# Weight sums of batch 0 on GpSimd, x turned in another order, gate inverses in step 0

## What is computed

```
xn = layernorm(x)
q, k, v = xn @ Wq.T, xn @ Wk.T, xn @ Wv.T      # 32 query heads, 8 key/value heads, 128 wide
q, k = rmsnorm(q) * q_norm_w, rmsnorm(k) * k_norm_w
attn = softmax(q k^T / sqrt(128) + alibi bias, causal)      # 4 query heads share a key head
s = (attn v) @ Wo.T
g = silu(xn @ W.T + bias + lora part)
out = x + s * g
```

## Time and profile before

| | |
|---|---|
| median of 3 runs | 2909.21 us (2906.86 to 2913.39) |
| the profiled execution | 2908.81 us, span 2906.9 us |
| TensorE busy, weight loads | 2658.3 us (91%), 2341.4 us (81%) |
| VectorE, ScalarE, GpSimd busy | 1741.1 (60%), 1771.0 (61%), 1684.1 us (58%) |
| HBM traffic | 151 GB/s over the span |
| granted TensorE clock, mean | 0.963 of full speed |

### The profile page before, as it was taken

How to read it: one execution, slowest core, us unless ns; L and a number is a source line. 1 busy time by engine, 2 the same in 40 slices (tenths; PEclk the granted TensorE clock), 3 DMA queues, 4 the chain that set the end, 5 groups by cost and what they waited for, 6 DMA issues and landing times.

```text
span 2906.9 us, 39948 instructions
## 1 busy us (share of the span) xinstructions
PE 2658.3 (91%) x13840; PEld 2341.4 (81%) x13840; DVE 1741.1 (60%) x3544; ACT 1771.0 (61%) x4627; POOL 1684.1 (58%) x821
## 2 busy tenths in 40 slices
PE   3668888888989999999989999999999999999997
PEld 2557777777878888888878888888877888888886
DVE  4445665556555666556656675655566575555566
ACT  2255555545666666666666666667666666766663
POOL 3366556656655576665555666566555665655643
PEclk8879999999999999999999999999999999999999
DMA  7767556665634433333423443333422543333323
GB/s 246 248 213 236 209 185 228 230 210 177 237 110 137 143 124 109 118 115 114 144 86 114 144 129 110 120 114 105 144 89 86 179 131 115 106 112 115 110 83 120
DMA packets 184119, 424.48 MB, mean 146 GB/s; under 512 B 34544, under 2 KB 75632, under 8 KB 183024
## 3 DMA queue, kind: packets, MB, share of 16 engines
q1 hardware_dynamic: 183920, 421.93, 44.4%
HBM read 349.51 MB, written 89.13 MB: 151 GB/s over the span
## 4 chain that ended last, share of the span: by engine, by line
PE 74%; DVE 8%; DMA 5%; ACT 5%; POOL 4%; SPq 3%; issue 3%; POOLq 0%; DVEq 0%; ACTq 0%
PE proj L477 18%; PE proj L479 17%; PE proj L478 17%; PE tr L570 4%; PE sc L477 3%; DMA wu<-xtok 3%; PE sc L478 2%; PE sc L479 2%; PE ot L478 2%; PE ot L479 2%; PE tr L550 2%; PE ot L477 2%; POOL wl L913 2%; SPq L295 1%; DVE pT_lo L1093 1%
## 5 line engine op out<-in xcount | busy, mean ns | idle before, releaser
L913 POOL TENSOR_TENSOR wl<-wl,wh 128x896 fp32r<-128x896 f32 x448 | 986.9, 2232 | 720.6 <-ACT wh L696 720.4
L477 PE MATMUL proj<-wh,xh 128*128 128x448 f32 x1792 | 679.9, 379 | 84.3 <-POOL wl L913 59.7
L478 PE MATMUL proj<-wl,xh 128*128 128x448 f32 x1792 | 665.6, 371 | 0.0
L479 PE MATMUL proj<-wh,xl 128*128 128x448 f32 x1792 | 665.2, 371 | 0.0
L924 POOL TENSOR_TENSOR wb_lo<-wb_lo,wb_hi 128x1024 fp32r<-128x1024 f32 x128 | 307.8, 2404 | 414.2 <-ACT wb_hi L706 414.2
L763 ACT ACTIVATE prob<-prob,negmax 128x128 f32<-128x128 f32 (+3 forms) x512 | 286.6, 564 | 339.9 <-DVE negmax L1128 339.9
L1150 DVE TENSOR_TENSOR acc<-acc,proj 128x512 f32<-128x512 f32 x480 | 327.5, 683 | 216.1 <-PE proj L479 214.4
L696 ACT ACTIVATE wh<-wl 128x896 fp32r<-128x896 f32 x448 | 406.8, 964 | 79.3 <-DMA wl<-wu 79.1
L477 PEld LDWEIGHTS proj<-wh,xh 128*128 128x128 f32 x1792 | 342.6, 191 | 123.6 <-issue 67.7
L477 PE MATMUL proj<-o_hi,wb_hi 128*128 128x512 f32 x1024 | 428.4, 418 | 12.3 <-issue 6.1
L479 PE MATMUL proj<-o_hi,wb_lo 128*128 128x512 f32 x1024 | 407.2, 398 | 0.0
(11 more groups left out here) (121 smaller groups left out, 4498.0 us busy)
## 6 DMA issues: line engine op xcount, KB each, us to landing
wl<-wu SPq DMA_DIRECT2D x448, 448.0 KB, 3.9
wb_lo<-wo_in SPq DMA_DIRECT2D x128, 512.0 KB, 3.3
wu<-xtok SPq DMA_DIRECT2D x98, 448.0 KB, 4.4
wo_in<-wo SPq DMA_DIRECT2D x32, 512.0 KB, 5.5
xtok<-wa SPq DMA_DIRECT2D x56, 256.0 KB, 4.1
gate_dram<-z_buf SPq DMA_DIRECT2D x32, 256.0 KB, 5.1
xtok<-wa SPq DMA_DIRECT2D x56, 128.0 KB, 4.1
xtok<-xT SPq DMA_DIRECT2D x28, 256.0 KB, 5.2
```

Of the source, the lines that this page charges most:

```text
L477: pe.matmul(out, hi_l, hi_r, start=first, stop=False, skip_group_check=onto)
L478: pe.matmul(out, hi_l, lo_r, start=False, stop=False, skip_group_check=onto)
L479: return pe.matmul(out, lo_l, hi_r, start=False, stop=last, skip_group_check=onto)
L913: pool.tensor_tensor(w_slot(wl, w), w_slot(wl, w, True), w_slot(wh, w), ALU.subtract).then_inc(w_ready, 1)
```

## The change

Four edits, all of them of order and place; the amount of TensorE's work stays.

1. The weight sums of half 0 in the steps pass from VectorE to GpSimd, into step j=1 ahead of the low parts of P4 and P5. On SP, `store_sums`, the landing wait and the twelve loads now stand ahead of `load_product` in j=0 and j=2, `store_halves` ahead of it in j=1.
2. x: another order of the fills and other sums (P6's goes to r21 rather than r22, and P5, P3 read it there), fills 0 to 3 in (6,3), 4 to 9 in (7,0), 10 to 13 in (7,1), some of them behind quarters of the output product; `x_sum` stands around `low_b` in (7,0) and (7,1). VectorE takes each fill's low part a piece later.
3. Layer norm: for batches 2 and 3 statistics and factors a group earlier, all four scalings in (6,1); x is loaded in g=3. For batch 1 two scalings move behind P3's pieces in (6,3).
4. Gate: the four inverses in j=0 (in j=1 for g=7 with a batch to come), the product always in j=1. `store_result(·, 0)` goes from j=2 to j=1, `finish` ahead of the low parts.

```
-FILLS = [P4, P1, P2, P6, P7, P5, P3]
-FILL_AT = {P1: (0, 0), P2: (0, 512), P4: (2, 512), P7: (2, 0), P6: (2, 512), P5: (0, 0), P3: (0, 512)}
+FILLS = [P1, P2, P7, P4, P6, P5, P3]
+FILL_AT = {P1: (0, 0), P2: (0, 512), P7: (2, 0), P4: (2, 512), P6: (2, 0), P5: (0, 0), P3: (0, 512)}
...
-    at = {(6, 3): range(0, 4), (7, 0): range(4, 8), (7, 1): range(8, 12), (7, 2): range(12, 14)}
+    at = {(6, 3): range(0, 4), (7, 0): range(4, 10), (7, 1): range(10, 14)}
...
+def ln_group(b):
+    return 6 if b == 1 else 5
```

On SP, in `step` at j = 0:

```
-                    load_product(n + 1, P6)
-                    load_product(n + 1, P7)
                     if new is not None:
                         sp.wait_ge(prep_tst[1], 64 * new)
                         load_weights(new, 0)
                         load_gate_weights(new, 0)
+                    load_product(n + 1, P6)
+                    load_product(n + 1, P7)
```

At j = 1:

```
-                    load_product(n + 1, P4)
                     if new is not None:
                         store_halves(new, 0)
+                    load_product(n + 1, P4)
+                    if g == 0 and ending is not None:
+                        store_result(ending, 0)
                     load_product(n + 1, P5)
```

At j = 2:

```
-                    if g == 0 and ending is not None:
-                        store_result(ending, 0)
-                    load_product(n + 1, P3)
...
                     if new is not None:
                         store_sums(new, 0)
                         sp.wait_ge(prep_tst[0], 64 * (new + 1))
                         load_weights(new, 1)
                         load_gate_weights(new, 1)
+                    load_product(n + 1, P3)
```

At j = 3:

```
-                    if g == 5 and 0 < b < BATCH - 1:
+                    if g == 3 and 0 < b < BATCH - 1:
                         load_x(b + 1)
```

On TensorE, in `turn_x` and `step`:

```
-                    pe.wait_ge(ln_ready, 4 * b + (2 if p == P4 else 4))
+                    pe.wait_ge(ln_ready, 4 * b + (4 if p == P4 else 2))
...
                 if v >= 0:
                     out_ready(v)
-                    out_proj(v, 0)
-                    out_proj(v, 1)
+                    for c in range(2):
+                        out_proj(v, c)
+                        if fills:
+                            turn_x(fills.pop(0))
```

On ScalarE, in `step`:

```
-                if (g, j) == (6, 3) and b + 1 < BATCH:
-                    ln_scale(b + 1, 0)
-                    ln_scale(b + 1, 1)
...
+                    if (g, j) == (6, 3) and b == 0 and u[1] == P3:
+                        ln_scale(1, 2 + u[2])
...
+                while fills:
+                    x_hi(fills.pop(0))
+                if (g, j) == (6, 1) and 0 < b < BATCH - 1:
+                    for t in range(NT):
+                        ln_scale(b + 1, t)
                 for k in range(3):
                     probs_hi(m, k)
-                if (g, j) == (6, 1) and b + 1 < BATCH:
+                if (g, j) == (ln_group(b + 1), 1) and b + 1 < BATCH:
                     ln_rsqrt(b + 1)
-                if (g, j) == (6, 2) and b + 1 < BATCH:
-                    ln_scale(b + 1, 2)
-                    ln_scale(b + 1, 3)
+                if (g, j) == (6, 2) and b == 0:
+                    ln_scale(1, 0)
+                    ln_scale(1, 1)
```

On GpSimd, in `step`:

```
                 bias_of(m + 1)
+                if next_x is not None:
+                    if (g, j) == (7, 0):
+                        x_sum(next_x, P7)
+                    if (g, j) == (7, 1):
+                        x_sum(next_x, P5)
                 low_b(v + 1)
+                if next_x is not None:
+                    if (g, j) == (7, 0):
+                        x_sum(next_x, P6)
+                    if (g, j) == (7, 1):
+                        x_sum(next_x, P3)
                 if j == 0:
                     values_lo(n)
-                if (g, j) == (6, 3) and b + 1 < BATCH:
-                    x_sum(b + 1, P7)
-                if j == 3 and n + 2 < HKV:
-                    weight_sums(n + 2)
-                low_product(*[(n + 1, P6), (n + 1, P4), (n + 1, P3), (n + 2, P1)][j])
-                if (g, j) == (6, 3) and b + 1 < BATCH:
-                    x_sum(b + 1, P6)
-                if (g, j) == (7, 0) and b + 1 < BATCH:
-                    x_sum(b + 1, P5)
-                if (g, j) == (7, 1) and b + 1 < BATCH:
-                    x_sum(b + 1, P3)
+                if j in (1, 3) and n + 2 < HKV:
+                    weight_sums(n + 2, j // 2)
                 if g == 0 and b > 0 and j in (1, 3):
                     finish(b - 1, j // 2)
+                low_product(*[(n + 1, P6), (n + 1, P4), (n + 1, P3), (n + 2, P1)][j])
```

On VectorE, in `step` (with `late_gate = g == 7 and next_x`):

```
                 for i, u in enumerate(pieces):
                     p, t = u[1:]
                     if p not in (P1, P2):
                         take_piece(*u)
+                    if turned:
+                        x_lo(turned.pop(0))
                     if fills:
-                        x_lo(fills.pop(0))
+                        turned.append(fills.pop(0))
+                    if (j, p, t) == (0, P2, 0):
+                        gate_sum(n)
...
+                if j == 0 and not late_gate:
                     for quarter in range(4):
                         gate_inverse(n, quarter)
-                late_gate = ending or (g == 6 and next_x)
+                turned += fills
+                if turned:
+                    x_lo(turned.pop(0))
                 add_out(v, 0)
+                if turned:
+                    x_lo(turned.pop(0))
...
-                if n + 2 < HKV:
-                    if j == 1:
-                        weight_sum(n + 2, 0, P5)
-                        weight_sum(n + 2, 0, P7)
-                    if j == 2:
-                        weight_sum(n + 2, 0, P6)
-                        weight_sum(n + 2, 0, P4)
```

More of the change, by code:

```diff
@@ L658, in step @@
                 pieces, fills = unit_pieces(n, j), x_fills(n, j)
-                while len(fills) > len(pieces):
-                    turn_x(fills.pop(0))
                 for u in pieces:
@@ L862, in step @@
                 pieces, fills = unit_pieces(n, j), x_fills(n, j)
-                while len(fills) > len(pieces):
-                    x_hi(fills.pop(0))
                 for u in pieces:
@@ L952, in x_sum @@
+                    pool.tensor_tensor(r11, r21, r11, ALU.add).then_inc(sum_ready, 1)
+                if what == P3:
                     pool.wait_ge(tr_done, TR["x", b, 3] + 1)
[L953 to L959, removed]
[L960 to L967 removed]
+                    pool.tensor_tensor(r12, r12, r21, ALU.subtract).then_inc(sum_ready, 1)
@@ new lines, in weight_sums @@
+            def weight_sums(g, h):
+                b11, b12, b21, b22 = (prep_tile(g, h, a, c) for a in range(2) for c in range(2))
+                c = 4 * g
+                pool.wait_ge(prep_bst[h], 48 * (g + 1))
+                pool.tensor_tensor(b11, b12, b11, ALU.subtract).then_inc(prep_t[h], 1)
+                pool.tensor_tensor(b12, b22, b12, ALU.subtract).then_inc(prep_t[h], 1)
+                pool.wait_ge(prep_t[h], c + 1)
+                pool.tensor_tensor(b22, b22, b11, ALU.subtract).then_inc(prep_t[h], 1)
+                pool.wait_ge(prep_t[h], c + 3)
+                pool.tensor_tensor(b21, b21, b22, ALU.subtract).then_inc(prep_t[h], 1)
@@ L1259, in step @@
                     queries_lo(n + 1, 0)
-                pieces, fills = unit_pieces(n, j), x_fills(n, j)
-                while len(fills) > len(pieces):
-                    x_lo(fills.pop(0))
                 if j == 0:
@@ L1266, in step @@
                     scale_rows("q3")
-                    gate_sum(n)
-                if j == 2 and g == 6 and next_x:
+                if j == 2 and g == ln_group(b + 1) and next_x:
                     ln_factors(b + 1)
+                late_gate = g == 7 and next_x
+                pieces, fills = unit_pieces(n, j), x_fills(n, j)
+                turned = []
                 for i, u in enumerate(pieces):
@@ L1273, in step @@
                         take_piece(*u)
+                    if turned:
+                        x_lo(turned.pop(0))
                     if fills:
-                        x_lo(fills.pop(0))
-                    if j == 1 and g == 6 and next_x:
+                        turned.append(fills.pop(0))
+                    if (j, p, t) == (0, P2, 0):
+                        gate_sum(n)
+                    if j == 1 and g == ln_group(b + 1) and next_x:
                         ln_stats(b + 1, (i,))
-                    elif j == 1 and ending:
+                    if j == 1 and ending:
                         result(b - 1, i)
-                    elif j == 1:
+                    if j == 1 and late_gate:
                         gate_inverse(n, i)
@@ L1285, in step @@
                         scale_rows("q1")
-                if j == 1 and not more:
+                if j == 0 and not more:
+                    gate_sum(n)
+                if j == 0 and not late_gate:
                     for quarter in range(4):
```

(14 more changed lines are left out.)

25 lines of the change are left out of this document (6 added, 19 removed).

## The result

The changed kernel takes 2837.35 us (median of four runs, 2834.12 to 2841.24), the kernel before on the same chip 2909.61: a ratio of 0.975, 95% interval 0.973 to 0.977. That is 72 us less. The forecast was 111 us less: the measured time lies outside the forecast's own bounds (2770 to 2828) and inside the wider range that takes in the rivals (2750 to 2848). The profiled execution took 2837.16 us, span 2835.3; it is set against the 2908.8 us of the prediction.

What follows compares the result with a forecast made beforehand. TensorE is full inside batches and loses time only in batch 0, mainly behind VectorE's late maxima, and at the borders. 2908.8 less 64.4 (batch 0) and 46.2 (borders) gives 2798 us, bounds 2770 to 2828, with rivals 2750 to 2848.

Steps and rivals of the forecast that it cites:

- (b): Batch 0: GpSimd becomes the bound, P4 coming 4 us past its cover in each of six groups; 2832 us, chance 0.10.
- (c): Borders: x's new order only trades waits, so they still lose 107 us; 2844 us, chance 0.10.
- Part 1, the sums on GpSimd: Batch 0: sums take 9.0 us a group off VectorE and add 8.4 on GpSimd in j=1, filling its idle 8.11.
- The cover of 2.4 us: After j=1: P4's first half is ready on GpSimd at 1140.8, 2.4 us before TensorE wants it.
- the contact with `gate_product`: Batch 0, j=1: this VectorE operation meets GpSimd's sums and takes longer; 0 to 1.9 us, 0.8 a group taken.
- Part 2, SP's order: Batch 0: products queue behind the landing wait; late P3 costs 5.3 us plus 2.6 of clock, late P6 0.8, a group.
- stores for 6.8 (421.5 to 428.3): SP in j=2 of batch 0: the stores take 6.8 us until landed, ahead of the loads and P3.
- The clock behind a wait: Batch 0, j=3: slower clock behind a 5.3 us wait costs 1.6 at least, twice that with two stretches; 2.6 taken.
- Part 3, the borders: The three borders between batches lose 60.9 us instead of 107.1, a gain of 46.2.
- The two new waits: Borders, (7,0) and (7,1): TensorE's fills 4 and 10 wait for GpSimd's sums of x, 4.0 us each, 5.6 with clock.
- (a): Batch 0: stores and loads overlap so well that P3 lands before ScalarE asks; 80 us a group, 2751 us, chance 0.10.
- (d): Batch 0: SP's ring delays P3 and P6, legs 2.2 times as long; slower than before, 2924 us, chance 0.04.

Runs made afterwards that it cites:

- the stores first: Against the changed kernel, stores of the sums issued at the head of SP's steps j=0 and j=2, ahead of output-weight load and copy: 2781.0 us (0.954).
- the copy last: Against the changed kernel, SP's DRAM-to-DRAM copy of the output weights moved from the head of each step to its end: 2805.5 us (0.964).

## Why the prediction was partly right

**The outcome:** right in direction and inside the wider range, but not inside the forecast's own bounds: the gain was to be 111 us and is 72. That the time lies next to those of rivals (b), 2832, and (c), 2844, says nothing for them; neither mechanism came.

**What bounds the kernel:** right. Groups inside batches kept their 78.8; all of the gain came from batch 0 and the borders. By stretches, in us against before: up to (6,2) of batch 0 -27.7 (forecast -64.4), the three borders -48.8, of which some 2.2 only went to (5,2), where the layer norm's factors now are (forecast -46.2), the last group +2.5 (forecast 0, -2 to +2; before 81.5, after 84.0; the other kernels with after's gate code there scatter from 81.4 to 84.3).

**Part 1, the sums on GpSimd:** right. The sums take 2.13 each and TensorE waits for nothing in j=2 behind them. The cover of 2.4 us held. Of the contact with `gate_product` nothing is to be seen in j=1's waits; j=2 is 0.3 longer, where 0.8 was taken.

**Part 2, SP's order:** the mechanism right, a size wrong, and here the forecast lost 34 us. The step that failed is "stores for 6.8 (421.5 to 428.3)". That leg was read from the chain of before, where VectorE's sums were late and the stores were issued after the output weights' load and copy had long been served. In the new order all three are issued within 1 us, and the leg is 9.5 in j=2 and 10.3 in j=0, in the mean. Issuing was right (6.1, forecast 6.0); the landing of the product took 5.4 in j=2 and 5.2 in j=0, a little more than the 4.6 taken. P3's first part landed 22.4 us after the step's start (21.1 to 23.9 in the five groups), not 18.5, and the wait in j=3 became 8.8 in place of 5.3; P6's landed after 22.7, not 18.5, which turned "0 to 1.5, I take 0.8" into 3.7 and 1.4 of clock. With the stores first the leg was 6.7, and a group took 85.0.

A second thing in Part 2 was never asked: whether the order was needed. The forecast costed it as it stood and did not ask what the sums' move alone would bring. The run with SP's order of before shows that this part of the change costs some 20 us, while the sums' move brings 50.

**The clock behind a wait:** 2.6 was taken behind a wait of 5.3 us. In j=3 it is 2.1 behind 8.8 us, 2.0 behind 6.5 with the copy last and 1.8 behind 3.9 with the stores first; in (7,0) it is 1.6 behind 3.9 at the first border, 2.9 at the second. So the size was right, and it hardly grows with the wait.

**Part 3, the borders:** right, in the sum and in its terms. A border loses 58.3 + 2.2 = 60.5 in the three together, against 60.9. The two new waits were to be 4.0 each and are 3.9 and 3.6 or 3.7; moving the sums gave 29 to 36 us in place of 33.6, with 1.4 us of wait left in each (7,1). The inverses' place alone is worth 29 us at the borders.

**The rivals:** (a), no wait of the ring, didn't come, but the loads in the landing wait make it so, and that kernel takes 2758.8, where (a) had 2751, a group 80.7, where (a) had 80. (b) was near in time (2832) and wrong in its reason: no wait on GpSimd's low parts in the five groups. (c) is excluded by the borders. (d) had the right quantity: legs 2.2 times as long were its price, and one leg of the three became 1.4 times as long.

## What to carry to other kernels

A landing time read from a trace holds for the place in the queue that it was read in. Before a store or load is moved, look at what would stand directly ahead of it, and add that. A wait in SP's queue is a place to put loads that are ready, while a load behind the wait inherits all of it. And a change of several parts is priced part by part against the kernel without that part: here one of three parts gave back 20 of the 90 us that the others brought.

## What the runs showed of the hardware

- Four stores of 448 KB each took 9.9, 8.6 and 6.7 us, with a load of 0.5 MB and a DRAM to DRAM copy of 0.5 MB, the load alone, or nothing issued directly ahead in the same queue. A wait for stores also waits for what is ahead of them.
- Some ten ns in the order of VectorE and GpSimd decide over 2 us: a VectorE operation of 0.68 us on two SBUF operands took 2.56 to 2.67 in ten groups of three kernels, where GpSimd's of 2.1 had begun 0.02 to 0.12 earlier; where it had begun 0.01 or 0.02 earlier, or came later, VectorE's took 0.68 and GpSimd's 2.6 to 2.7. The Trainium skill (SBUF — State Buffer, Who interferes with whom) calls the shared port pair an exclusive lock; the trace agrees. With the keys' scaling moved ahead, that one took 0.68 (293.14), and the next such operation, in j=3 beside the second low part of P3, took 1.8 in its turn. In the changed kernel that one took 2.1 in four of the five groups (1.5 in the fifth), where it cost TensorE nothing.
- Of TensorE's 120 steps with a wait of 3.1 us or more in these thirteen profiles, 118 were run in part at the lower of the two clock levels (1.2 GHz). Of the 64 steps whose longest wait was between 1.8 and 3.1 us, 55 were; of the 177 with waits of 0.15 to 1.8 us alone, 31 were, and 146 kept 2.4 GHz throughout.
